# A transformer block on eight cores: a ScalarE copy of the reciprocal row in the weight preparation, and one fewer buffer ahead of the second matmul

## The chip, the cores and the metric

The kernel runs on one Trainium2 chip, as the same program on all 8 cores (two dies, cores 0 to 3 and 4 to 7). Each core takes 4096 tokens: 3967 of the inactive part and 129 of the last 516 of a sequence, in which attention reaches the output. The metric is the device time in microseconds (us) of the slowest core. There is no communication between cores, so each core runs its own program from start to end and the slowest one sets the time.

## What is computed

`x` is 2 x 16384 x 1024. The reference, cut to what matters here:

```python
x = x + layernorm(attention(layernorm(x)))     # 16 heads, 4 sinks + a window of 512
def bitlinear(x, w):
    scale = clip(mean(abs(w), axis=1), 1e-5)
    tern = clip(round(w / scale), -1, 1)
    return x @ (tern * scale).T
h = bitlinear(xn, w_fc) + gate * (xn @ v.T @ fast_b.T @ u.T)   # 1024 -> 4096
r = maximum(h, 0)
x = x + layernorm(bitlinear(r * r, w_proj))                    # 4096 -> 1024
```

## The kernel before

Every engine has its own instruction list, written by hand in program order by the emitter `E`. All instructions are issued from one helper (L114), so the profile shows L114 for nearly all, and the tile names tell the groups apart. `E.gset(key, sem)` notes a semaphore count at which a buffer is free, `E.gwait(eng, key)` makes an engine wait for it. Engines work strictly in the order in which their instructions were emitted. There are two stages.

**Stage 1, to about 1420 us: attention and weight preparation.** After the layer norms of the context, 32 attention units (8 for K, 8 for Q, 16 heads) are emitted, and behind each one two weight preparation units, 64 in all (L824 to L834): 32 of `mk_fc` (L716) for `w_fc`, then 32 of `mk_pj` (L768) for `w_proj`. A unit loads 128 x 1024 weights into one half of `stg`, sums their absolute values in `emit_wsum` (L665: twice a ScalarE Relu into `sgn`, a VectorE pass into `lnscr`, and four matmuls with ones into the PSUM banks `ST` and `pb4`), reduces the sums on VectorE to a row `srowp`, and takes its reciprocal. TensorE then spreads the reciprocal row over 128 partitions into `ST[:, 128:256]` (`mk_pj`: 32 columns), and transposes the scale into `ST[:, 384:385]`. ScalarE copies the scale into `hsc` (`mk_pj`: `osch`), VectorE waits for that copy and multiplies the staged weights in place with the spread row, which it reads from PSUM (L746, L796; `mk_fc` also scales its part of `u2T`, L749). Two more VectorE passes write the ternary weights into `Sfc` or `Spj`. `ST` is noted free behind the multiplication. Next comes the following unit, whose first VectorE pass stands behind all of this on VectorE.

**Stage 2, from about 1420 us: the feed-forward part,** in 16 tiles of 256 tokens. For each of 32 hidden chunks h, f(h) (`emit_fc`, L979) is 8 matmuls `pb<-xn,Sfc` into one of two banks (`pbig0`, `pbig1`), a Relu with scale into `rpp` (ScalarE for even h, VectorE for odd h) and a VectorE multiplication into `r2s`; that frees the bank, so f(h) waits for the multiplication of chunk h-2. p(h) (`emit_proj`, L1016) is 8 matmuls `pb<-r2s,Spj` that add chunk h to four output banks. `r2s` is a ring of 6 buffers and p runs 6 chunks behind f: TensorE's list in a tile is

f(0) to f(3) (`fc_head`, emitted behind the last p of the tile before), f(4), f(5), S, Z, then p(h-6), f(h) for h = 6 to 31, then p(26) to p(31).

S is the 8 matmuls `pb<-fsq,cvecb` of the second layer norm of the tile before; they need `fsq`, which ScalarE and VectorE make from the four output banks of that tile behind its p(31) and behind its followers' chunks 0 to 3 (L1112 to L1146). Z is 4 matmuls `pb<-zrow` of 1 x 512 zeros that clear the output banks (L1071). The rest of the layer norms of the tile before and of the next tile is tied to fixed h: the rows of the second norm at h = 7, its broadcast at 9, its two passes at 11 and 13, the sum with x, the store and the load of `xtl` for the tile after next at 15, the first layer norm of the next tile from h = 18 to 29.

Of the kernel before, what the change touches and what calls it, by code (L numbers as in the profile page):

```python
# [7 lines left out]
F32 = mybir.dt.float32  # L8
BF16 = mybir.dt.bfloat16
AF = mybir.ActivationFunctionType  # L10
ALU = mybir.AluOpType
# [14 lines left out]
TT = 256  # L26
NTILE = TOK // TT
DCN = D // 128
HCN = HF // 128
# [89 lines left out]
def build_nc(n_tiles=NTILE):  # L119
# [29 lines left out]
    with ExitStack() as octx:  # L149
# [7 lines left out]
        srowp = sbuf("srowp", [1, 384], F32)  # L157
        hsc2 = sbuf("hsc2", [128, NFC], F32)
        osch = sbuf("osch", [128, OCN], F32)
        fbTf = sbuf("fbTf", [16, R], F32)  # L160
        fbTg = sbuf("fbTg", [16, R], BF16)
        gatef = sbuf("gatef", [1, 1], F32)
        g2c = sbuf("g2c", [16, 1], F32)
        lnscr = sbuf("lnscr", [128, 4096], BF16)
        zrow = sbuf("zrow", [1, 512], BF16)
        cvec = sbuf("cvecs", [128, 8], F32)
        cvecb = sbuf("cvecb", [128, 8], BF16)
        crow = sbuf("crows", [1, 128], F32)
# [161 lines left out]
        with ExitStack() as actx:  # L330
# [385 lines left out]
            def mk_fc(ph, sg, sgk):  # L716
              def unit():
                slot = ph % 2
                stflat = stg[:, slot * 1024:slot * 1024 + 1024]
                st3 = stg3a if slot == 0 else stg3b  # L720
                E.gwait("sync", f"stg{slot}")
                cL = E.dma("sync", stflat,
                           t_wfc[ph * 128:(ph + 1) * 128, :], f"dS{slot}")
                E.gwait("scalar", sgk)
                E.wait("scalar", f"dS{slot}", cL)
                E.gwait("tensor", "ST")
                cRw = emit_wsum(stflat, sg, 4, 128, 1.0 / D)
                E.wait("scalar", "sV", cRw)
                E.op("scalar", "activation", srowp[0:1, 256:384],
                     srowp[0:1, 0:128], AF.Square, inc="sA")  # L730
                cH2 = E.cnt["sA"]
                E.wait("tensor", "sA", cH2)
                E.op("tensor", "matmul", ST[:, 128:256], crow[:],
                     srowp[0:1, 128:256], start=True, stop=True)
                E.op("tensor", "transpose", ST[:, 384:385],
                     srowp[0:1, 256:384], idf1, inc="sP")
                cBc = E.cnt["sP"]
                E.gset("srowp", "sP")
                E.wait("scalar", "sP", cBc)
                E.op("scalar", "activation", hsc2[:, ph:ph + 1],  # L740
                     ST[:, 384:385], AF.Copy, inc="sA")
                hsc_ready.append(E.cnt["sA"])
                E.wait("vector", "sA", hsc_ready[-1])
                E.wait("vector", "sP", cBc)
                rb3 = ST[:, 128:256].unsqueeze(1).broadcast_to((128, DCN, 128))
                E.op("vector", "tensor_tensor", st3, st3, rb3, ALU.mult)  # L746
                if ph == 0:
                    E.wait("vector", "dGi", c_dG_init)
                E.op("vector", "tensor_tensor",  # L749
                     u2T[0:16, ph * 128:(ph + 1) * 128],  # L750
                     u2T[0:16, ph * 128:(ph + 1) * 128],
                     ST[0:16, 128:256], ALU.mult, inc="sV")
                cZ = E.cnt["sV"]
                E.gset("ST", "sV")
                E.drain("vector")
                E.op("vector", "tensor_single_scalar", sg,
                     stflat, -0.5, ALU.is_lt, inc="sV")
                E.drain("vector")
                E.op("vector", "scalar_tensor_tensor",
                     sfc3[:, :, ph * 128:(ph + 1) * 128], st3, 0.5,  # L760
                     sg.rearrange("p (c t) -> p c t", c=DCN),
                     ALU.is_gt, ALU.subtract, inc="sV")
                sfc_ready.append(E.cnt["sV"])
                E.gset(f"stg{slot}", "sV")
                E.gset(sgk, "sV")
              return unit

            def mk_pj(po, sg, sgk):  # L768
              def unit():
                slot = po % 2  # L770
                stflat = stg[:, slot * 1024:slot * 1024 + 1024]
                stp3 = stflat.rearrange("p (c t) -> p c t", c=HCN)
                E.gwait("sync", f"stg{slot}")
                cL = E.dma("sync", stflat,
                           t_wpj[po * 128:(po + 1) * 128, :], f"dS{slot}")
                E.gwait("scalar", sgk)
                E.wait("scalar", f"dS{slot}", cL)
                E.gwait("tensor", "ST")
                cRw = emit_wsum(stflat, sg, 16, 32, 1.0 / HF)
                E.wait("tensor", "sV", cRw)  # L780
                E.op("tensor", "matmul", ST[:, 128:160], crow[:],
                     srowp[0:1, 128:160], start=True, stop=True)
                E.op("tensor", "transpose", ST[0:32, 384:385],
                     srowp[0:1, 0:32], idf1, inc="sP")
                cBc = E.cnt["sP"]
                E.gset("srowp", "sP")
                E.wait("scalar", "sP", cBc)
                oc = po // 4
                rlo = 32 * (po % 4)
                E.op("scalar", "activation", osch[rlo:rlo + 32, oc:oc + 1],  # L790
                     ST[0:32, 384:385], AF.Copy, inc="sA")
                osch_ready.append(E.cnt["sA"])
                E.wait("vector", "sA", osch_ready[-1])
                E.wait("vector", "sP", cBc)
                rb3 = ST[:, 128:160].unsqueeze(1).broadcast_to((128, HCN, 32))
                E.op("vector", "tensor_tensor", stp3, stp3, rb3, ALU.mult,  # L796
                     inc="sV")
                cZ = E.cnt["sV"]
                E.gset("ST", "sV")
                E.drain("vector")  # L800
                E.op("vector", "tensor_single_scalar", sg,
                     stflat, -0.5, ALU.is_lt, inc="sV")
                E.drain("vector")
                E.op("vector", "scalar_tensor_tensor",
                     spj3[:, :, po * 32:(po + 1) * 32], stp3, 0.5,
                     sg.rearrange("p (c t) -> p c t", c=HCN),
                     ALU.is_gt, ALU.subtract, inc="sV")
                spj_ready.append(E.cnt["sV"])
                E.gset(f"stg{slot}", "sV")
                E.gset(sgk, "sV")  # L810
              return unit
# [99 lines left out]
        with ExitStack() as bctx:  # L911
# [3 lines left out]
            fsq = bsb("fsq", [128, DCN * 512], BF16)  # L915
            fscr = stg
            E.gset("fscr", "sV")
            r2s = [bsb(f"r2s{i}", [128, TT], BF16) for i in range(6)]
            rpp = [bsb(f"rpp{i}", [128, TT], F32) for i in range(2)]

            xn3_t = [v3(x, TT) for x in xn_t]
# [57 lines left out]
            def emit_fc(j, hc):  # L979
# [10 lines left out]
                if hc % 2 == 0:  # L990
# [5 lines left out]
                         bank[:, 0:TT], AF.Relu,  # L996
                         scale=hsc2[:, hc:hc + 1], inc="sA")
                    cR = E.cnt["sA"]
                    E.gwait("vector", f"r2s{hc % 6}")
                    E.wait("vector", "sP", cF)  # L1000
                    E.wait("vector", "sA", cR)
                else:
# [3 lines left out]
                         bank[:, 0:TT], hsc2[:, hc:hc + 1], 0.0,  # L1006
                         ALU.mult, ALU.max)
                    E.drain("vector")
                    E.gwait("vector", f"r2s{hc % 6}")
                E.op("vector", "tensor_tensor", r2s[hc % 6][:],  # L1010
                     bank[:, 0:TT], rpp[hc % 2][:], ALU.mult, inc="sV")
                r2_of[j][hc] = E.cnt["sV"]
                E.gset(key, "sV")
# [2 lines left out]
            def emit_proj(j, hc):  # L1016
                E.wait("tensor", "sV", r2_of[j][hc])
                for oc in range(OCN):
                    bank = pbk[2 + oc // 2]
                    E.op("tensor", "matmul",  # L1020
                         bank[:, (oc % 2) * TT:(oc % 2) * TT + TT],
                         s_pj[:, hc * D + oc * 128:hc * D + oc * 128 + 128],
                         r2s[hc % 6][:], start=False,
                         stop=(hc == HCN - 1 and oc % 2 == 1),
                         inc=("sP" if oc == OCN - 1 else None))
                E.gset(f"r2s{hc % 6}", "sP")

            def fc_head(j):
                r2_of[j] = [0] * HCN
# [31 lines left out]
            ln1 = None  # L1061
            for j in range(n_tiles):
                emit_fc(j, 4)
                emit_fc(j, 5)
                if pend2 is not None:
                    adv(pend2)
                for bnk in range(4):
                    E.gwait("tensor", f"pbproj{bnk}")
                    if j == 0 and bnk == 0:
                        E.wait("tensor", "sV", c_spj)  # L1070
                    E.op("tensor", "matmul", pbk[2 + bnk][:, 0:512],  # L1071
                         zrow[0:1, 0:128], zrow[0:1, 0:512],
                         start=True, stop=False)
                for hc in range(6, HCN):
                    emit_proj(j, hc - 6)
                    emit_fc(j, hc)
                    if pend2 is not None:
                        if hc == 7:
# [25 lines left out]
                            E.gset("fscr", "sV")  # L1104
                            tile_state[j + 1] = ln1[1][0]
                E.gset(f"xn{j % 2}", "sP")
                for hc in range(HCN - 6, HCN):
                    emit_proj(j, hc)
                c_proj = E.cnt["sP"]
                if j + 1 < n_tiles:  # L1110
# [154 lines left out]
```

How the kernel before makes its waits and increments, by code:

```python
    def replay(self, eng_name, engobj, sems):  # L106
        for act in self.q[eng_name]:
            if act[0] == "w":
                engobj.wait_ge(sems[act[1]], act[2])
            elif act[0] == "d":
                engobj.drain()
            else:
                _, fname, args, kwargs, incv = act
                inst = getattr(engobj, fname)(*args, **kwargs)
                if incv is not None:
                    inst.then_inc(sems[incv[0]], incv[1])
```

## Time and profile before

| what | value |
|---|---|
| median of 2 runs | 2811.86 us (2809.02 to 2814.70) |
| profiled execution, its own time | 2807.6 us |
| its span on the slowest core (core 0) | 2806.1 us |
| spans of the other cores | 2768.6 to 2794.7 us |
| mean granted TensorE clock, core 0 | 0.706 (others 0.707 to 0.719) |
| TensorE matmul busy | 1653.1 us, 59% |
| TensorE weight load busy | 1080.6 us, 39% |
| VectorE busy | 1320.2 us, 47% |
| ScalarE busy | 479.3 us, 17% |

The profiled execution took 1.5 us more than its span, and is 4.3 us under the median. The clock is given as a share of 2.4 GHz; it has two levels, 1.0 and 0.5, and a mean between them says how much of a stretch lay at either. In rows of the trace a time in brackets is how long the engine had been idle before the group, with what it waited for. Names in a row are out<-in; `stg<-stg,pb` reads PSUM, `stg<-xtl,stg` reads only SBUF.

### The profile page before, as it was taken

The page shows a single profiled execution, that of the slowest core. Times are in us where ns is not written, and L with a number is a line of the kernel's source. Part 1 is how long each engine was busy: PE and PEld are TensorE (multiplying, and loading weights), DVE is VectorE, ACT ScalarE, POOL GpSimd, SP SyncE. Part 2 cuts the span into 40 slices and gives each one's busy share as a digit, 9 for nine tenths or more (in the row PEclk, how much of TensorE's full clock was granted, in tenths as well). Part 3 has the DMA queues.
Part 4 walks back from the last instruction along what each step waited for, and adds up shares of the span by engine and source line. Part 5 has one row for each costly group of instructions (what it writes and reads, how often), then busy time and mean ns, then how long its engine had stood idle before and what let it go on. Part 6 is the DMA issues. An engine that isn't in the chain of part 4 may idle for free.

```text
span 2806.1 us, 31767 instructions; the slowest of 8 cores (2768.6 to 2806.1 us)
## 1 busy us (share of the span) xinstructions
PE 1653.1 (59%) x10820; PEld 1080.6 (39%) x10824; DVE 1320.2 (47%) x2281; ACT 479.3 (17%) x1025; POOL 20.8 (1%) x36
## 2 busy tenths in 40 slices
PE   3433333333333333334588888888878887878886
PEld 1111111111111111111166656665666665656655
DVE  1244555455545445545444444444544444444544
ACT  1111111111111111121011111111112112111111
POOL 0000000000000000000000000000000000000000
PEclk8555555555555555555588888998999889989988
DMA  2101011101000100001101011100010001110000
GB/s 46 27 30 45 30 45 36 47 30 45 23 31 29 39 23 30 24 29 23 45 1 31 1 31 31 31 25 7 31 31 31 31 1 31 31 31 31 11 22 31
DMA packets 49199, 80.51 MB, mean 29 GB/s; under 512 B 12019, under 2 KB 37748, under 8 KB 48004
## 3 DMA queue, kind: packets, MB, share of 16 engines
q1 hardware_dynamic: 28244, 44.60, 5.4%
q0 software_dynamic: 4160, 17.11, 2.5%
q10 hardware_dynamic: 16640, 16.78, 2.2%
q8 instruction: 92, 1.51, 0.2%
q14 instruction: 63, 0.52, 0.1%
HBM read 70.42 MB, written 16.78 MB: 31 GB/s over the span
## 4 chain that ended last, share of the span: by engine, by line
PE 48%; DVE 27%; issue 9%; ACT 8%; DMA 7%; DVEq 1%; ACTq 0%; SPq 0%; POOLq 0%
PE pb L114 47%; DVE lnscr L114 7%; DVE srowp L114 5%; DMA xtl<-xT 5%; DVE stg L114 4%; DVE srow L114 4%; ACT sgn L114 3%; ACT srow L114 1%; ACT lnscr L114 1%; DVE r2s L114 1%; DVE sgn L114 1%; DVE fsq L114 1%; DVE nmb L114 1%; DVEq L109 1%; DVE Sfc L114 1%
## 5 line engine op out<-in xcount | busy, mean ns | idle before, releaser
L114 PE MATMUL pb<-xn,Sfc 128*128 128x256 bf16 x4096 | 570.0, 287 | 127.9 <-DVE r2s L114 121.3
L114 PE MATMUL pb<-r2s,Spj 128*128 128x256 bf16 x4096 | 561.9, 287 | 0.0
L114 PEld LDWEIGHTS pb<-xn,Sfc 128*128 128x128 bf16 x4096 | 412.0, 103 | 221.8 <-issue 155.0
L114 PEld LDWEIGHTS pb<-r2s,Spj 128*128 128x128 bf16 x4096 | 416.6, 103 | 97.1 <-issue 31.4
L114 DVE TENSOR_TENSOR r2s<-pb,rpp 128x256 bf16<-128x256 f32 x512 | 215.9, 424 | 499.3 <-ACT rpp L114 442.4
L114 PE MATMUL pb<-sgn,cvecb 128*1 128x512 bf16 x256 | 129.5, 609 | 430.2 <-DVE lnscr L114 430.2
L114 DVE SCALAR_TENSOR_TENSOR lnscr<-stg,sgn 128x1024 bf16<-128x1024 f32 x128 | 156.6, 1223 | 297.3 <-ACT sgn L114 297.3
L114 ACT ACTIVATE rpp<-pb,hsc 128x256 f32<-128x256 f32 x256 | 122.1, 477 | 919.7 <-PE pb L114 905.7
L114 PE MATMUL pb<-lnscr,cvecb 128*1 128x512 bf16 x472 | 206.6, 566 | 66.4 <-ACT lnscr L114 65.5
L114 PEld LDWEIGHTS pb<-sgn,cvecb 128*1 128x1 bf16 x256 | 14.5, 80 | 495.0 <-issue 495.0
L114 DVE TENSOR_TENSOR stg<-stg,pb 128x1024 f32<-128x1024 f32 (+1 forms) x96 | 151.1, 1573 | 97.0 <-ACT hsc L114 56.4
L114 ACT ACTIVATE sgn<-stg 128x1024 bf16<-128x1024 f32 x128 | 134.9, 1054 | 316.1 <-PE pb L114 315.6
L114 DVE TENSOR_SCALAR rpp<-pb,hsc 128x256 f32<-128x256 f32 x256 | 122.6, 479 | 88.8 <-PE pb L114 85.8
L114 PE MATMUL pb<-srowp,crows 1*128 1x128 f32 (+1 forms) x128 | 43.6, 437 | 199.9 <-ACT srowp L114 118.6
L114 DVE TENSOR_REDUCE srowp<-pb 1x128 f32<-1x512 f32 (+1 forms) x128 | 81.7, 674 | 136.6 <-PE pb L114 136.6
L114 PEld LDWEIGHTS pb<-srowp,crows 1*128 1x128 f32 x128 | 31.7, 305 | 257.5 <-issue 257.5
L114 PEld LDWEIGHTS pb<-lnscr,cvecb 128*1 128x1 bf16 x472 | 51.8, 113 | 181.3 <-issue 169.4
L114 PE MATMUL pb<-srow,crows 1*128 1x256 f32 (+3 forms) x172 | 59.2, 479 | 94.3 <-DVE srow L114 94.3
L114 PE MATMUL pt<-identb,lnscr 1*128 1x1 bf16 (+3 forms) x160 | 17.5, 232 | 116.5 <-DVE lnscr L114 116.5
L114 PEld LDWEIGHTS pb<-srow,crows 1*128 1x128 f32 x172 | 37.2, 254 | 117.1 <-issue 113.4
L114 DVE TENSOR_TENSOR srow<-srow 1x256 f32<-1x256 f32 (+3 forms) x129 | 46.9, 363 | 58.3 <-ACT srow L114 49.4
L114 DVE TENSOR_SCALAR srow<-pb 1x256 f32<-1x256 f32 (+3 forms) x86 | 27.4, 354 | 94.1 <-PE pb L114 93.9
(102 smaller groups left out, 1208.5 us busy)
## 6 DMA issues: line engine op xcount, KB each, us to landing
stg<-wfc_st SPq DMA_DIRECT2D x32, 512.0 KB, 3.5
stg<-wpj_st SPq DMA_DIRECT2D x32, 512.0 KB, 3.5
outT<-stg ACTq DMA_DIRECT2D x16, 1024.0 KB, 10.2
xtl<-xT SPq DMA_DIRECT2D x16, 512.0 KB, 6.6
xtl<-xT POOLq DMA_DIRECT2D x16, 512.0 KB, 9.8
ctxXg<-ctxT SPq DMA_DIRECT2D x8, 256.0 KB, 2.9
wbuf<-wk POOLq DMA_DIRECT2D x2, 1024.0 KB, 11.1
wbuf<-wq POOLq DMA_DIRECT2D x2, 1024.0 KB, 8.8
```

The costliest lines, as they stand in the source:

```text
L109: engobj.wait_ge(sems[act[1]], act[2])
L114: inst = getattr(engobj, fname)(*args, **kwargs)
```

## The change

In both preparation units ScalarE now also copies the spread reciprocal row from `ST` into a new SBUF buffer `rbb` (two slots of 128 columns), `ST` is noted free behind this copy, and VectorE waits for the copy and reads `rbb` in its multiplications. To have the room (1 KB for each partition), the ring `r2s` goes from 6 buffers to 5, with p running 5 chunks behind f, and `zrow` from 512 to 256 elements, with two matmuls of 256 columns for each bank in Z.

```diff
+        rbb = sbuf("rbb", [128, 256], F32)
-        zrow = sbuf("zrow", [1, 512], BF16)
+        zrow = sbuf("zrow", [1, 256], BF16)
@@ mk_fc
                 E.wait("scalar", "sP", cBc)
+                E.gwait("scalar", f"rbb{slot}")
                 E.op("scalar", "activation", hsc2[:, ph:ph + 1],
                      ST[:, 384:385], AF.Copy, inc="sA")
                 hsc_ready.append(E.cnt["sA"])
-                E.wait("vector", "sA", hsc_ready[-1])
-                E.wait("vector", "sP", cBc)
-                rb3 = ST[:, 128:256].unsqueeze(1).broadcast_to((128, DCN, 128))
+                E.op("scalar", "activation", rbb[:, slot * 128:slot * 128 + 128],
+                     ST[:, 128:256], AF.Copy, inc="sA")
+                cRb = E.cnt["sA"]
+                E.gset("ST", "sA")
+                E.wait("vector", "sA", cRb)
+                rb3 = rbb[:, slot * 128:slot * 128 + 128].unsqueeze(
+                    1).broadcast_to((128, DCN, 128))
                 E.op("vector", "tensor_tensor", st3, st3, rb3, ALU.mult)
...
-                     ST[0:16, 128:256], ALU.mult, inc="sV")
+                     rbb[0:16, slot * 128:slot * 128 + 128], ALU.mult,
+                     inc="sV")
-                E.gset("ST", "sV")
+                E.gset(f"rbb{slot}", "sV")
@@ mk_pj: the same with 32 columns
@@ feed-forward part
-            r2s = [bsb(f"r2s{i}", [128, TT], BF16) for i in range(6)]
+            r2s = [bsb(f"r2s{i}", [128, TT], BF16) for i in range(5)]
...
                 emit_fc(j, 4)
-                emit_fc(j, 5)
...
-                    E.op("tensor", "matmul", pbk[2 + bnk][:, 0:512],
-                         zrow[0:1, 0:128], zrow[0:1, 0:512],
+                    E.op("tensor", "matmul", pbk[2 + bnk][:, 0:256],
+                         zrow[0:1, 0:128], zrow[0:1, 0:256],
                          start=True, stop=False)
-                for hc in range(6, HCN):
-                    emit_proj(j, hc - 6)
+                    E.op("tensor", "matmul", pbk[2 + bnk][:, 256:512],
+                         zrow[0:1, 0:128], zrow[0:1, 0:256],
+                         start=False, stop=False)
+                for hc in range(5, HCN):
+                    emit_proj(j, hc - 5)
                     emit_fc(j, hc)
...
-                for hc in range(HCN - 6, HCN):
+                for hc in range(HCN - 5, HCN):
                     emit_proj(j, hc)
```

TensorE's list around the end of a tile, in the kernel before (`xn,Sfc` are the matmuls of f, `r2s,Spj` those of p, `fsq` is S, `zrow` is Z):

```order
L114 MATMUL pb<-r2s,Spj 128x256 x48
L114 MATMUL pb<-xn,Sfc 128x256 x48
L114 MATMUL pb<-fsq,cvecb 1x512 x8
L114 MATMUL pb<-zrow 128x512 x4
L114 MATMUL pb<-r2s,Spj 128x256 x8
L114 MATMUL pb<-xn,Sfc 128x256 x8
```

and at the same place in the changed kernel:

```order
L114 MATMUL pb<-r2s,Spj 128x256 x40
L114 MATMUL pb<-xn,Sfc 128x256 x40
L114 MATMUL pb<-fsq,cvecb 1x512 x8
L114 MATMUL pb<-zrow 128x256 x8
L114 MATMUL pb<-r2s,Spj 128x256 x8
L114 MATMUL pb<-xn,Sfc 128x256 x8
```

One f, f(5), has moved from ahead of S to behind Z and p(0); behind f(31) there are five p where there were six. VectorE's and ScalarE's lists are unchanged in this stage.

ScalarE's list in the preparation, the difference from the kernel before at two neighbouring `mk_fc` units (`sgn<-stg` are the Relus of `emit_wsum`, `hsc` is the copy of the scale):

```order
 L114 ACTIVATE srowp<-srowp 1x128 [waits sV]
-L114 ACTIVATE hsc<-pb 128x1 [waits sP]
-L114 ACTIVATE sgn<-stg 128x1024 [waits sV,dS1]
-L114 ACTIVATE sgn<-stg 128x1024 [waits sP]
-L114 ACTIVATE srowp<-srowp 1x128 [waits sV]
-L114 ACTIVATE hsc<-pb 128x1 [waits sP]
+L114 ACTIVATE hsc<-pb 128x1 [waits sP,sV]
+L114 ACTIVATE rbb<-pb 128x128
+L114 ACTIVATE sgn<-stg 128x1024 [waits sV,dS1]
+L114 ACTIVATE sgn<-stg 128x1024 [waits sP]
+L114 ACTIVATE srowp<-srowp 1x128 [waits sV]
```

The copy stands between `hsc` and the next unit's Relu, and `hsc` has one more wait, for the slot of `rbb`. On VectorE no instruction is added or moved; its multiplication waits for ScalarE alone where it waited for ScalarE and TensorE.

## Rows read from the trace of the kernel before

**Rows 1.** Part 2 of the page: 40 slices of the span, in tenths.
```profile
PE   3433333333333333334588888888878887878886
PEclk8555555555555555555588888998999889989988
```
**Rows 2.** Timeline, one `mk_fc` unit: start us, us, engine, operation [idle before <-releaser].
```profile
319.32 0.17 ACT L114 ACTIVATE hsc<-pb 128x1 f32<-128x1 f32 x1 [1.01 <-PE pb L114]
...
319.66 1.22 DVE L114 TENSOR_TENSOR stg<-stg,pb 128x1024 f32<-128x1024 f32 x1 [1.75 <-ACT hsc L114]
...
321.97 1.23 DVE L114 SCALAR_TENSOR_TENSOR Sfc<-stg,sgn 128x1024 bf16<-128x1024 f32 x1
323.12 1.22 DVE L114 SCALAR_TENSOR_TENSOR lnscr<-stg,sgn 128x1024 bf16<-128x1024 f32 x1
...
324.58 1.01 PE L114 MATMUL pb<-sgn,cvecb 128*1 128x512 bf16 x2 [5.36 <-DVE lnscr L114]
```
**Rows 3.** Groups by form, VectorE: count | busy us, mean ns | idle before.
```profile
L114 DVE TENSOR_TENSOR stg<-stg,pb 128x1024 f32<-128x1024 f32 x64 | 78.1, 1221 | 94.6 <-ACT hsc L114 56.4 <-ACT osch L114 38.2
L114 DVE TENSOR_TENSOR stg<-stg,pb 128x2048 f32<-128x2048 f32 x32 | 72.9, 2278 | 2.4 <-PE pb L114 2.3
L114 DVE TENSOR_SCALAR sgn<-stg 128x1024 bf16<-128x1024 f32 x64 | 44.4, 694 | 6.8
L114 DVE TENSOR_TENSOR stg<-xtl,stg 128x2048 f32<-128x2048 f32 x16 | 36.7, 2292 | 1.7
L114 DVE TENSOR_TENSOR lnscr<-xtl 128x1024 bf16<-128x1024 f32 x16 | 19.5, 1218 | 0.0
```
**Rows 4.** ScalarE: two neighbours of a timeline, then two groups by form.
```profile
716.75 0.28 ACT L114 ACTIVATE lnscr<-pb 128x129 bf16<-128x129 f32 x1 [1.64 <-PE pb L114]
716.92 1.05 ACT L114 ACTIVATE sgn<-stg 128x1024 bf16<-128x1024 f32 x1
...
L114 ACT ACTIVATE lnscr<-pb 128x64 bf16<-128x64 f32 x64 | 8.2, 198 | 0.0
...
L114 ACT ACTIVATE osch<-pb 32x1 f32<-32x1 f32 x32 | 5.1, 159 | 210.8 <-PE pb L114 210.8
```
**Rows 5.** Timeline across the end of one tile.
```profile
2014.51 5.40 PE L114 MATMUL pb<-r2s,Spj 128*128 128x256 bf16 x48
...
2019.75 1.91 PE L114 MATMUL pb<-xn,Sfc 128*128 128x256 bf16 x16
...
2024.31 2.12 PE L114 MATMUL pb<-xn,Sfc 128*128 128x256 bf16 x16 [0.26 <-DVE r2s L114]
2024.82 0.42 DVE L114 TENSOR_TENSOR r2s<-pb,rpp 128x256 bf16<-128x256 f32 x1 [0.17 <-DVE rpp L114]
2025.16 1.65 DVE L114 TENSOR_SCALAR stg<-pb,osch 128x256 f32<-128x256 f32 x4
...
2029.30 1.89 PE L114 MATMUL pb<-fsq,cvecb 128*1 128x512 bf16 x8 [2.88 <-DVE fsq L114]
2031.12 1.03 PE L114 MATMUL pb<-zrow 1*128 1x512 bf16 x4
2032.09 1.05 PE L114 MATMUL pb<-r2s,Spj 128*128 128x256 bf16 x8
```
**Rows 6.** Chain of waits through the tile behind it: start us, us, what.
```profile
2029.30 7.34 PE pb L114 x52
...
2054.20 2.30 DVE stg L114
...
2057.05 11.98 DMA xtl<-xT
```
**Rows 7.** TensorE in 11.1 us from each S: stretch, length, busy (x), granted clock, DMA.
```profile
1497.80:1508.90 11.10, 11.10 (x43) 0.54 0.00 0
...
1944.60:1955.70 11.10, 11.05 (x58) 0.69 0.01 2
2029.30:2040.40 11.10, 9.95 (x77) 1.00 0.00 0
```

More of the change, by code:

```diff
@@ L787, in unit @@
                 E.wait("scalar", "sP", cBc)
+                E.gwait("scalar", f"rbb{slot}")
                 oc = po // 4
@@ L792, in unit @@
                 osch_ready.append(E.cnt["sA"])
-                E.wait("vector", "sA", osch_ready[-1])
-                E.wait("vector", "sP", cBc)
-                rb3 = ST[:, 128:160].unsqueeze(1).broadcast_to((128, HCN, 32))
+                E.op("scalar", "activation", rbb[:, slot * 128:slot * 128 + 32],
+                     ST[:, 128:160], AF.Copy, inc="sA")
+                cRb = E.cnt["sA"]
+                E.gset("ST", "sA")
+                E.wait("vector", "sA", cRb)
+                rb3 = rbb[:, slot * 128:slot * 128 + 32].unsqueeze(
+                    1).broadcast_to((128, HCN, 32))
                 E.op("vector", "tensor_tensor", stp3, stp3, rb3, ALU.mult,
@@ L798, in unit @@
                 cZ = E.cnt["sV"]
-                E.gset("ST", "sV")
+                E.gset(f"rbb{slot}", "sV")
                 E.drain("vector")
@@ L998, in emit_fc @@
                     cR = E.cnt["sA"]
-                    E.gwait("vector", f"r2s{hc % 6}")
+                    E.gwait("vector", f"r2s{hc % 5}")
                     E.wait("vector", "sP", cF)
@@ L1008, in emit_fc @@
                     E.drain("vector")
-                    E.gwait("vector", f"r2s{hc % 6}")
-                E.op("vector", "tensor_tensor", r2s[hc % 6][:],
+                    E.gwait("vector", f"r2s{hc % 5}")
+                E.op("vector", "tensor_tensor", r2s[hc % 5][:],
                      bank[:, 0:TT], rpp[hc % 2][:], ALU.mult, inc="sV")
@@ L1022, in emit_proj @@
                          s_pj[:, hc * D + oc * 128:hc * D + oc * 128 + 128],
-                         r2s[hc % 6][:], start=False,
+                         r2s[hc % 5][:], start=False,
                          stop=(hc == HCN - 1 and oc % 2 == 1),
                          inc=("sP" if oc == OCN - 1 else None))
-                E.gset(f"r2s{hc % 6}", "sP")
+                E.gset(f"r2s{hc % 5}", "sP")
             def fc_head(j):
```

## The prediction

> **What bounds the kernel now.** I read the page's slices first. They show two stages [rows 1]. For the first 19 of 40 slices TensorE is busy about three tenths of the time at the lower clock level, 1.2 GHz; from then on it is busy eight tenths and the clock is mostly at 2.4 GHz. The change has a part in each, so I price each stage by itself.
>
> In the first stage the timeline of one preparation unit shows a single chain from engine to engine [rows 2]. VectorE's multiplication starts 0.17 us after `hsc` ends (319.32 + 0.17 = 319.49, start 319.66), having been idle 1.75 us. From there VectorE runs without a gap to its pass for the next unit at 323.12, and TensorE waits for that pass. So whatever delays the multiplication delays everything behind it, in the second unit of a pair as shown, and in the first, where the attention unit's VectorE work is queued behind it.
>
> In the second stage I read the timeline across the end of a tile [rows 5]. TensorE runs p(26) to p(31) as 48 matmuls, then f(0) to f(5) in pairs, and is then idle for 2.88 us until `fsq` is ready. That wait does not depend on f(4) or f(5): `fsq` comes from VectorE's evacuation (2025.16), which stands behind the multiplication of chunk 3 (2024.82). Behind S the chain is TensorE up to f(7), then the layer norm's rows, later the sum with x at 2054.20, and a load of `xtl` that ends last [rows 6]. All of these hang on f(7), f(15) and f(18), not on absolute time. Last I read the granted clock in the 11.1 us behind each S [rows 7].
>
> **Part 1: the copy into `rbb`.** It adds 64 ScalarE instructions, each between `hsc` (or `osch`) and the multiplication. On ScalarE a neighbour starts before the one ahead has ended: 716.92 against an end at 716.75 + 0.28 = 717.03, so 0.11 us early [rows 4]. The copy therefore starts 0.17 - 0.11 = 0.06 us after `hsc`. The nearest row in size is the 128x129 copy from PSUM, 0.28 us; the copy ends 0.34 us after `hsc` started, where `hsc` ended after 0.17: +0.17 us for each `mk_fc`, 32 x 0.17 = 5.4 us. For `mk_pj` `osch` takes 0.16, the copy starts 0.05 later, and with 32 columns takes a little under the 0.198 of the 128x64 row, say 0.18: it ends at 0.23, +0.07, 32 x 0.07 = 2.2 us. Together 8 us, all on the chain. VectorE's multiplication loses one of two waits and `hsc` gains one (for the slot, released two units earlier); I count these against each other. Bounds: below, if the whole gap of 0.17 us ahead of the multiplication went with the second wait, 64 x 0.17 = 11 us off, so -3 us. Above, if the copy didn't overlap and took 0.31 and 0.20 us from the end of `hsc` or `osch`, 32 x 0.31 + 32 x 0.20 = 16 us. I take 8, the row nearest in size.
>
> What the copy could give: the multiplication reads SBUF twice instead of SBUF and PSUM. It takes 1221 ns now; a VectorE product of the same size from SBUF alone takes 1218, and at 2048 columns the PSUM form takes 2278 and the SBUF form 2292 [rows 3]. So nothing, within 14 ns x 64 = 1 us. The earlier release of `ST` also gives nothing: the next matmul into `ST` needs VectorE's pass into `lnscr` too, which stands behind the multiplication and two more passes on the same engine [rows 2]. The next unit's Relu is up to 0.2 us later on ScalarE, behind which VectorE is still busy for over 2 us.
>
> The Trainium skill, page "VectorE: DVE Perf Modes", section on the TRN2 errata, gives a VectorE operation a fixed 120 cycles from PSUM and 58 from SBUF. By it, as an estimate, each multiplication would be 0.065 us shorter, about 4 us for 64, and the part would cost 4 us instead of 8. The rows above don't bear it out, so the measured durations stand.
>
> **Part 2: the ring of 5.** Inside a tile it costs nothing: before p(h-5) can come up, f(h-1) has waited for the multiplication of chunk h-3, which is later than h-5, so p never waits; and f(h) still waits for chunk h-2. At the end of a tile p(29) to p(31) come one p earlier behind f(31), but three p's (2.6 us) still lie ahead of p(30).
>
> The cost is at S. With f(5) moved behind it, TensorE reaches S one f earlier and waits longer. One f is 8 matmuls at (2019.75 - 2014.51) / 48 = 0.109 us, 0.87 us [rows 5], so the wait goes from 2.88 to about 3.75 us. From S to f(7) there is now one f and one p more (+1.75 us), from f(31) to the end of p(31) one p fewer (-0.87). Since the norm's steps, the store and the load are tied to f, they all move by 1.75, and nothing in between absorbs it. Net +0.87 us at each of 15 boundaries: 13 us. The first tile has no S and the last S has no f ahead of it.
>
> **Part 3: Z.** Four matmuls take 2032.09 - 2031.12 = 0.97 us now; eight of 256 columns at 0.109 would take 0.87 us [rows 5]. Between -0.1 and, if each added one cost another 0.1, +0.3 us a tile: -2 to +5 us; I take 0.
>
> **Part 4: the clock behind the longer wait.** The 15 stretches of 11.1 us behind S show a granted clock of 1.00 three times, 0.85 to 0.87 twice, 0.69 nine times and 0.54 once; three of the 15 stand in [rows 7]. A mean of 0.69 is (1 - 0.69) / 0.5 = 62% of the stretch at 1.2 GHz, 6.9 us, in which half the work is lost: 3.4 us. TensorE had been idle for 2.88 us ahead of each of them, so a wait of this length sometimes drops the clock and sometimes doesn't, and a longer one can only do so more often. I take two of the three stretches at full clock as lost, 2 x 3.4 = 7 us. Bounds: -7 us, if the phases fall better, to +37 us: a fall to 0.54 at all 15, where 0.54 costs (1 - 0.54) x 11.1 = 5.1 us and the present mean costs (9 x 3.4 + 2 x 1.6 + 5.1) / 15 = 2.6.
>
> The Trainium skill, page "TensorE: Matmul & The Clock Gate", section on HAM oscillation, says that idle gaps between bursts of matmuls put the clock back to its half rate, and that the loss is paid again in each round of a loop. The trace agrees in kind (12 of 15 boundaries). By that rule all 15 would lose, which makes it the rival "clock" below.
>
> **Sum.** 8 + 13 + 0 + 7 = 28 us on the profiled execution's 2807.6 us (span 2806.1 and 1.5 us around it): 2835.6. The median shown lies 4.3 us above that execution, so the forecast is 2840 us, 1.0% over 2811.86.
>
> **The rivals.**
> - *Absorbed.* The moved f costs nothing, because a later wait takes it in, such as the one for the load of `xtl` in the middle of the tile. For it speaks that this load is on the chain with 11.98 us; against it, that it starts behind the sum with x at h = 15, so both ends move [rows 6]. Then only the copy counts: 2812 + 8 = 2820 us.
> - *SBUF is faster.* The multiplication might reach the rate of the one-input row, 694 ns in place of 1221 [rows 3]: 64 x 0.53 = 34 us saved, and with the 28 the time is 2812 + 28 - 34 = 2806 us. Against it stand both SBUF rows with two inputs.
> - *Clock.* The place is S in every tile, the price is the upper bound of part 4. It decides if a wait of 3.75 us drops the clock every time, where one of 2.88 us left it alone at three boundaries of 15, and if the clock then needs as long to come back as at 1497.8: 8 + 13 + 37 = 58 us, 2870 us, 2.1% slower.
> - *No use for the release.* That `ST` is free earlier without anyone who takes it is part of the forecast already; if someone did, it would show as a shorter first stage, with a floor near 2815 us. I give it nothing of its own beyond the range.
>
> **How the numbers follow.** Forecast 0.72, absorbed 0.12, clock 0.10, SBUF faster 0.06. The forecast's own range is 2825 to 2858 (copy -3 to 16 and clock -7 to +20, not all at once). The range for 8 times in 10 takes in the absorbed case and stops short of the clock rival: 2818 to 2864. A measurement of this kernel can tell about 2% (56 us) from no change. Slower by more than that: nearly half of the clock rival and a little of the forecast's tail, 0.07. Faster by more than 2% has no case, 0.01. Within 2%: 0.92.
>
> **What would show it.** Right: a row `rbb<-pb` of 0.28 to 0.31 us x32 and one near 0.18 x32; the multiplication's idle time up from 1.75 to about 1.9 us, its duration still 1.22; TensorE's wait for `fsq` near 3.75 us at 15 boundaries; S to S longer by 0.87 us at equal clock; the stage up to the first Z longer by 8 us. Wrong: a multiplication well under 1.2 us, a wait at S that stays at 2.88, p groups that wait for `r2s`, or a stage 2 as long as before.

## The result and the profile after

The changed kernel takes 2883.04 us (median of 11 runs, 2858.98 to 2923.49) where the kernel before takes 2809.06 us (10 runs): the ratio is 1.0269, with a 95% interval of 1.0227 to 1.0311, 2.7% slower. The forecast was 2840 us, 1.0% slower, and the range ended at 2864; the "clock" rival gave 2870. The ratio is taken without the few executions, such as the one of 2923.49, in which the cores of one die ran longer at a lower granted clock than the other die. The profiled execution of the changed kernel took 2864.0 us and lies near the fast end of its runs, so its trace shows 56 us of the 74 by which the medians differ. On the mean of the eight cores the spans of the two profiled executions differ by 61 us. Pairs of traces are compared below as means over all eight cores where that is said.

The head of the page, which answers to [rows 1]:

```profile
span 2862.5 us, 31962 instructions; the slowest of 8 cores (2823.0 to 2862.5 us)
...
PEclk8555555555555555555588888888888888888888
```

In the second stage no slice reaches nine tenths of the full clock any more, where nine did. The clock in the first stage looks as before.

One preparation unit of core 0, timeline (start us, us, engine, operation, idle before), which answers to [rows 2]:

```profile
306.89 0.17 ACT L114 ACTIVATE hsc<-pb 128x1 f32<-128x1 f32 x1 [1.07 <-PE pb L114]
306.96 0.27 ACT L114 ACTIVATE rbb<-pb 128x128 f32<-128x128 f32 x1
...
307.33 1.23 DVE L114 TENSOR_TENSOR stg<-stg,rbb 128x1024 f32<-128x1024 f32 x1 [1.91 <-ACT rbb L114]
```

The copy starts 0.07 us after `hsc` and takes 0.27 us; the multiplication waits for it, 1.91 us idle in place of 1.75. In three of four units of the second kind (`mk_pj`) the copy starts later than expected:

```profile
710.92 0.16 ACT L114 ACTIVATE osch<-pb 32x1 f32<-32x1 f32 x1 [6.63 <-PE pb L114]
711.10 0.20 ACT L114 ACTIVATE rbb<-pb 128x32 f32<-128x32 f32 x1
711.40 1.23 DVE L114 TENSOR_TENSOR stg<-stg,rbb 128x1024 f32<-128x1024 f32 x1 [1.39 <-ACT rbb L114]
```

Groups by form of core 2, which answer to the first of [rows 3] (count | busy us, mean ns | idle before):

```profile
L114 DVE TENSOR_TENSOR stg<-stg,rbb 128x1024 f32<-128x1024 f32 x64 | 78.4, 1225 | 105.3 <-ACT rbb L114 105.3
...
L114 PE MATMUL pb<-fsq,cvecb 128*1 128x512 bf16 x128 | 57.1, 625 | 65.5 <-DVE fsq L114 60.6 <-ACT stg L114 4.8
```

The multiplication takes 1225 ns, no less than the 1221 from PSUM, and its idle time went from 94.6 to 105.3 us: 11 us for the copy. The second row is S: a mean of 625 ns for one matmul.

The end of a tile on TensorE, core 2, which answers to [rows 5]:

```profile
1511.11 1.03 PE L114 MATMUL pb<-xn,Sfc 128*128 128x256 bf16 x8 [0.25 <-DVE r2s L114]
1516.11 3.57 PE L114 MATMUL pb<-fsq,cvecb 128*1 128x512 bf16 x8 [3.96 <-DVE fsq L114]
1519.61 1.88 PE L114 MATMUL pb<-zrow 1*128 1x256 bf16 x8
1521.43 1.89 PE L114 MATMUL pb<-r2s,Spj 128*128 128x256 bf16 x8
```

The wait ahead of S is 3.96 us where it was 2.88, and S takes 3.57 us where it took 1.89. Behind it Z (1.88) and the first p (1.89) are at half rate too. The stretches of 11.1 us behind S of the same core, which answer to [rows 7] (stretch, length, busy (x), granted clock, DMA):

```profile
1516.11:1527.21 11.10, 11.10 (x56) 0.63 0.00 0
...
2771.30:2782.40 11.10, 11.10 (x52) 0.58 0.01 1
```

All 15 of this core lie between 0.58 and 0.64. Over the eight cores 99 of 120 lie between 0.54 and 0.64 and 21 between 0.85 and 0.88, and none at 1.00. I counted the boundaries of all eight cores, 120 of them, by the time from S to the next norm's broadcast at h = 9. At full clock it is 11.1 us in the order of before (12.86 in the changed order, which has one f and one p more in it). In the kernel before 73 of 120 are longer than that, with a mean of 12.92, so 1.8 us are lost at a boundary. In the changed kernel all 120 are longer, with a mean of 16.61: 3.75 us lost.

Means over eight cores, from S to S: 85.4 us before, 88.8 after, +3.4 for each of 15 boundaries or 50 us. The first Z comes at 1431.5 before and 1439.7 after, +8. Of the 50 us, 13 are the moved f (0.87 each) and 29 are the clock between S and the broadcast (3.75 - 1.82 = 1.93 each). The slow stretch doesn't end there: from the broadcast to the wait for `xtl` it is 24.4 us in place of 23.4, with 2.8 us at half clock in place of 0.7, another 15 us in all. The wait for `xtl`, which comes next, is 4.9 us in place of 5.4 and takes back 7 of them, so 8 are left.

### The profile page after: what moved, and what is told of

Same layout as the page of the kernel before. It is cut to its first block, busy times and chain, and to the rows that moved or that the text cites. A ratio compares the mean times of both kernels' runs of the same rounds, so it can differ in the third digit from the quotient of the medians.

```text
span 2862.5 us, 31962 instructions; the slowest of 8 cores (2823.0 to 2862.5 us)
## 1 busy us (share of the span) xinstructions
PE 1698.6 (59%) x10888; PEld 1109.0 (39%) x10888; DVE 1322.0 (46%) x2281; ACT 487.3 (17%) x1089; POOL 20.8 (1%) x36
## 4 chain that ended last, share of the span: by engine, by line
PE 49%; DVE 27%; issue 9%; ACT 8%; DMA 6%; DVEq 1%; ACTq 0%; SPq 0%; POOLq 0%
PE pb L114 49%; DVE lnscr L114 6%; DVE srowp L114 5%; DMA xtl<-xT 4%; DVE stg L114 4%; DVE srow L114 4%; ACT sgn L114 3%; DMA ctxXg<-ctxT 2%; ACT lnscr L114 1%; ACT srow L114 1%; DVE r2s L114 1%; DVE sgn L114 1%; DVE fsq L114 1%; DVE nmb L114 1%; DVE Sfc L114 1%
## 5 line engine op out<-in xcount | busy, mean ns | idle before, releaser
L114 PE MATMUL pb<-xn,Sfc 128*128 128x256 bf16 x4096 | 583.1, 291 | 101.0 <-DVE r2s L114 95.3
L114 PE MATMUL pb<-r2s,Spj 128*128 128x256 bf16 x4096 | 582.7, 293 | 0.0
L114 PEld LDWEIGHTS pb<-xn,Sfc 128*128 128x128 bf16 x4096 | 420.2, 104 | 197.5 <-issue 123.0
L114 PEld LDWEIGHTS pb<-r2s,Spj 128*128 128x128 bf16 x4096 | 425.1, 105 | 101.2 <-issue 27.7
L114 DVE TENSOR_TENSOR stg<-stg,rbb 128x1024 f32<-128x1024 f32 x64 | 78.4, 1225 | 105.3 <-ACT rbb L114 105.3
L114 PE MATMUL pb<-fsq,cvecb 128*1 128x512 bf16 x128 | 57.1, 625 | 65.5 <-DVE fsq L114 60.6
```

The source lines that it names most:

```text
L114: inst = getattr(engobj, fname)(*args, **kwargs)
```

## The experiments

Two theories were to be told apart. A: the longer wait at S drops the clock every time, and this is most of the loss. Against it stood B (the copy, or the split of Z), C (the new order itself, with waits that follow from it) and later D to F, each told where it is tested. "The wait at S" below is the mean over the 15 boundaries of a core, the same on all eight cores to 0.01 us. A boundary is called long if it takes over half a microsecond more from S to the broadcast than at full clock; that is 11.10 us in the order of before, 12.86 in the changed order, and 11.97 where p alone comes one step earlier (e3, e8, e9). Each ratio is to the kernel before, with its 95% interval. One thing made clean experiments possible: `r2s` lives only in stage 2, whose own buffers need less room for each partition than those of stage 1, so the ring of 6 fits beside `rbb`.

**e1_ring: the shorter ring alone.** Stage 1 and Z are those of the kernel before.

```diff
-            r2s = [bsb(f"r2s{i}", [128, TT], BF16) for i in range(6)]
+            r2s = [bsb(f"r2s{i}", [128, TT], BF16) for i in range(5)]
...
                 emit_fc(j, 4)
-                emit_fc(j, 5)
...
-                    emit_proj(j, hc - 6)
+                    emit_proj(j, hc - 5)
```

Expected: 

> The kernel before with the ring of 5 alone (f(5) behind Z), no copy, Z unsplit. Theory A, the clock falls behind every longer wait at S: most of the loss is here, +50 to +65 us on before, S at half clock (3.57 us) at nearly all 15 boundaries, wait at S 3.9 to 4.0 us. Rival B, the loss comes from the copy or from the split of Z: +13 us at most here.

Measured: 1.0261 (1.0216 to 1.0305). The boundary on core 0:

```profile
2036.92 3.57 PE L114 MATMUL pb<-fsq,cvecb 128*1 128x512 bf16 x8 [3.96 <-DVE fsq L114]
2040.42 1.88 PE L114 MATMUL pb<-zrow 1*128 1x512 bf16 x4
```

All but a few tenths of a per cent of the loss is in this part. The wait is 3.96 us, and all 120 boundaries are longer than at full clock, mean 16.67 us. The loss is 73 us (60 to 85), somewhat above the 50 to 65 that I had written down.

**e2_ring6: the copy and the split Z, with the ring of 6.** The changed kernel with the diff of e1 undone.

```diff
-            r2s = [bsb(f"r2s{i}", [128, TT], BF16) for i in range(5)]
+            r2s = [bsb(f"r2s{i}", [128, TT], BF16) for i in range(6)]
...
                 emit_fc(j, 4)
+                emit_fc(j, 5)
```

Expected: 

> The changed kernel with the ring back at 6 buffers and f(5) ahead of S; the copy and the split Z stay. Theory A: +10 to +15 us on before, wait at S 2.88 us again, S at full clock in some tiles. Rival B (copy or split Z): still +60 us or more.

Measured: 1.0051 (1.0029 to 1.0074), 14 us (8 to 21). The wait at S is 2.91 us, 88 of 120 boundaries are long, mean 13.34 us, and the first Z comes at 1441.3 us (mean of eight cores), 10 us later than before. B falls: what the copy costs is near its 10 us in the first stage, not 60.

**e6_zsplit: the split of Z alone.** The kernel before with two matmuls of 256 columns for each bank.

```diff
-                    E.op("tensor", "matmul", pbk[2 + bnk][:, 0:512],
-                         zrow[0:1, 0:128], zrow[0:1, 0:512],
+                    E.op("tensor", "matmul", pbk[2 + bnk][:, 0:256],
+                         zrow[0:1, 0:128], zrow[0:1, 0:256],
                          start=True, stop=False)
+                    E.op("tensor", "matmul", pbk[2 + bnk][:, 256:512],
+                         zrow[0:1, 0:128], zrow[0:1, 0:256],
+                         start=False, stop=False)
```

Expected: 

> The kernel before with the split of Z alone. All theories: Z takes 0.87 to 1.0 us in place of 0.97 at full clock, no change that can be told (within 5 us of before).

Measured: 1.0000 (0.9970 to 1.0029). Nothing, as said. The wait at S is that of the kernel before, 2.87 us, and yet 86 boundaries are long in this trace against 73: so far apart can two executions be with nothing changed at S.

**e4_fill24_after: the changed kernel, with TensorE kept at work in the wait.** 24 matmuls whose result nobody reads, into the PSUM bank `pt`, which stage 2 leaves unused, are put between f(4) and S. Order, copy and ring stay as changed.

```diff
                 if pend2 is not None:
+                    for _ in range(24):
+                        E.op("tensor", "matmul", ptf[:, 0:TT],
+                             s_fc[:, 0:128], xn_t[j % 2][:, 0:TT],
+                             start=True, stop=True)
                     adv(pend2)
```

Expected: 

> The changed kernel with 24 matmuls of 256 columns into the unused bank pt between f(4) and S, 2.6 us of TensorE work inside the wait. Theory A: the wait left at S is about 1.3 us, the clock stays at 1.0 through S, 45 to 65 us faster than the changed kernel, near +10 to +25 us on before or better. Rival C, the loss is the order itself (one f more behind S) and waits that follow from it, not the clock: no faster than the changed kernel.

Measured: 0.9949 (0.9918 to 0.9979), 3.1% under the changed kernel by the two ratios. Core 0:

```profile
2018.40 2.78 PE L114 MATMUL pt<-xn,Sfc 128*128 128x256 bf16 x24
2022.78 1.89 PE L114 MATMUL pb<-fsq,cvecb 128*1 128x512 bf16 x8 [1.60 <-DVE fsq L114]
2024.60 1.04 PE L114 MATMUL pb<-zrow 1*128 1x256 bf16 x8
```

S starts no earlier, since it waits for `fsq`, but it runs in 1.89 us, and S to the broadcast takes 12.87 us on the mean of 120 boundaries, none of them long. Work was added and 3% went away, some 90 us where 45 to 65 had been expected. C falls, and A is shown: the clock was the cost. The gain passed what A had been given, because the kernel before loses at S as well.

**e4b_fill8_after: the same with 8 matmuls,** as many as f(5) has.

```diff
-                    for _ in range(24):
+                    for _ in range(8):
```

Expected: 

> The changed kernel with 8 such matmuls, as long as one f: the wait at S is back near 2.9 to 3.1 us, with the order of the change. Theory A: the clock behaves as in the kernel before (S at full clock in a fifth to half of the tiles), so the time is before + 10 (copy) + 13 (one f more), some 2830 us. Rival C: as slow as the changed kernel.

Measured: 1.0109 (1.0069 to 1.0149), 31 us (19 to 42) over the kernel before, where 23 had been expected. The wait at S is 3.16 us, 67 of 120 boundaries are long, mean 15.10. Where the clock does fall here, it costs more (4.0 us for a long boundary, 3.0 in the kernel before), as one boundary of core 0 shows:

```profile
2030.48 1.04 PE L114 MATMUL pt<-xn,Sfc 128*128 128x256 bf16 x8
2034.89 2.30 PE L114 MATMUL pb<-fsq,cvecb 128*1 128x512 bf16 x8 [3.37 <-DVE fsq L114]
2037.12 1.88 PE L114 MATMUL pb<-zrow 1*128 1x256 bf16 x8
```

**e3_f5_ahead: the order of TensorE repaired at S, with the ring of 5.** The 8 matmuls of f(5) go back ahead of S; only the VectorE part of chunk 5, which needs the buffer that p(0) frees, stays behind p(0). `emit_fc_mm` is the bank wait and the matmuls of `emit_fc`.

```diff
+            def emit_fc_mm(j, hc):
...
                 emit_fc(j, 4)
+                emit_fc_mm(j, 5)
                 if pend2 is not None:
                     adv(pend2)
```

Expected: 

> The changed kernel, ring of 5, copy and split Z kept, with only the 8 matmuls of f(5) moved back ahead of S (its VectorE work still waits for p(0)). Theory A: the wait at S is 2.88 us again and the time is that of the kernel with the ring of 6, before + 10 to 15 us. Rival D, the fifth buffer itself costs (VectorE waits for p(0), f(7) for VectorE): 10 us or more above the kernel with the ring of 6, and f(7) waits at each boundary.

Measured: 0.9986 (0.9959 to 1.0014). The wait at S is back at 2.91 us on core 0, and 55 of 120 boundaries are long. D falls: the fifth buffer costs nothing that can be told (within 0.3%), even with the copy in the kernel. A had 10 to 15 us over before for it, and it came out 4 under (11 under to 4 over); that made rival F, that p one step earlier is better by itself.

**e8_f5_ahead_nocopy: the same without the copy and with Z unsplit,** so that it differs from the kernel before only in the ring of 5 and in p coming one step earlier.

```diff
-            r2s = [bsb(f"r2s{i}", [128, TT], BF16) for i in range(6)]
+            r2s = [bsb(f"r2s{i}", [128, TT], BF16) for i in range(5)]
...
-                emit_fc(j, 5)
+                emit_fc_mm(j, 5)
```

Expected: 

> The kernel before with the ring of 5, p running 5 chunks behind f, and the matmuls of f(5) kept ahead of S; no copy, Z unsplit. Theory A, only the wait at S matters: same as before within 0.3%. Rival F, p one step earlier is better by itself (the kernel with copy and split Z in this form came out at 0.9986 of before although the copy costs about 10 us): 0.4 to 0.8% faster than before.

Measured: 0.9982 (0.9953 to 1.0011). That is A's answer; of F at most its lower end is left, 0.4% faster, which the interval takes in. The boundaries that are long are fewer, 45 of 120 against 73, and why is open. Open too is where the copy's cost went in e3: its first Z comes at 1443.1 us and here at 1432.2, 11 us apart, but the totals of the two differ by less than their intervals, and in the two traces e3 gets the time back in stage 2, mostly by shorter waits for `xtl` (4.9 against 5.7 us a tile).

**e5_fill24_before: the filler in the kernel before,** 24 matmuls between f(5) and S, with the same diff as e4.

Expected: 

> The kernel before with the 24 matmuls into the unused bank pt between f(5) and S. Theory A: the wait left at S is 0.3 us, S at full clock at 15 boundaries, S to the next rows of the norm 11.1 us everywhere (12.7 to 14.4 now): 25 to 40 us faster than before, 1.0 to 1.4%. Rival C: no change, or slower by the matmuls.

Measured: 0.9916 (0.9874 to 0.9957), 24 us (12 to 35), a little less than the 25 to 40 expected, though the trace shows at S just what was meant: wait 0.25 us, all 120 boundaries at 11.10 us. Core 4:

```profile
2016.89 1.89 PE L114 MATMUL pb<-fsq,cvecb 128*1 128x512 bf16 x8 [0.26 <-DVE fsq L114]
```

The mean loss at S was 1.82 us (12.92 - 11.10), and 15 x 1.82 = 27 us.

**e7_fill3_before: the filler at three waits of the kernel before.** `filler(j, n)` is n such matmuls. Beside the 24 ahead of S, as in e5:

```diff
                     emit_proj(j, hc - 6)
+                    if hc == 21 and j + 1 < n_tiles:
+                        filler(j, 36)
                     emit_fc(j, hc)
...
                         elif hc == 27:
+                            filler(j, 24)
                             adv(ln1[0])
```

Expected: 

> The same, with 36 more such matmuls ahead of f(21), where TensorE waits for the load of xtl, and 24 ahead of the broadcast of the first norm's rows at h = 27. Theory A: the half-clock stretches behind these two waits go as well, 1.5 to 3 us each a tile: another 25 to 60 us, 2.5% or more below before in all. Rival E: the longer dense load on all cores brings a lower granted clock on its own, or the load of xtl is already there in some tiles and the 36 matmuls are in the way: no better than with the filler at S alone.

Measured: 0.9688 (0.9647 to 0.9729), 2706 us, 3.1% faster than before and some 64 us under e5, where 25 to 60 had been expected. Core 0 at the wait for `xtl` and at S, and the page's clock:

```profile
2019.92 4.09 PE L114 MATMUL pt<-xn,Sfc 128*128 128x256 bf16 x36
2025.93 1.03 PE L114 MATMUL pb<-xn,Sfc 128*128 128x256 bf16 x8 [1.92 <-DVE r2s L114]
...
2062.52 2.78 PE L114 MATMUL pt<-xn,Sfc 128*128 128x256 bf16 x24
2065.56 1.89 PE L114 MATMUL pb<-fsq,cvecb 128*1 128x512 bf16 x8 [0.26 <-DVE fsq L114]
```

```profile
PEclk7555555555555555555559999999999999999998
```

The waits for `xtl` and for the rows are still there in length, only filled; what is gone is the half clock behind them. From S to S a tile takes 79.1 us on the mean of the cores, where the kernel before has 85.4. E, that the denser load lowers the granted clock by itself or that the fillers get in the way, falls: no slice of stage 2 but the last is under nine tenths.

**e9_fill3_ring5: e7 on the kernel of e8.** The three fillers, with the ring of 5 and f(5)'s matmuls ahead of S.

```diff
                 emit_fc_mm(j, 5)
                 if pend2 is not None:
+                    filler(j, 24)
                     adv(pend2)
...
                     emit_proj(j, hc - 5)
+                    if hc == 21 and j + 1 < n_tiles:
+                        filler(j, 36)
```

Expected: 

> That kernel with the three fillers (24 ahead of S, 36 ahead of f(21), 24 at h = 27). Theory A: as the kernel of six buffers with the fillers, 0.969 of before, within 0.2%. Rival F: clearly below it, 0.963 or less.

Measured: 0.9661 (0.9616 to 0.9706), 2703 us. A had 0.969 within 0.2% and F 0.963 or less; it lies between, and can't be told from e7. These two are the fastest versions of the study, and both beat the kernel before and the changed one.

The wait at S, the long boundaries of 120 in each trace, and the mean time that a boundary lost against full clock:

| kernel | mean wait at S, us | long ones | mean loss, us | ratio to before |
|---|---|---|---|---|
| e5_fill24_before | 0.25 | 0 | 0.0 | 0.9916 |
| e4_fill24_after | 1.42 | 0 | 0.0 | 0.9949 |
| before | 2.87 | 73 | 1.8 | 1 |
| e6_zsplit | 2.87 | 86 | 2.2 | 1.0000 |
| e8_f5_ahead_nocopy | 2.87 | 45 | 1.4 | 0.9982 |
| e2_ring6 | 2.91 | 88 | 2.2 | 1.0051 |
| e3_f5_ahead | 2.91 | 55 | 1.5 | 0.9986 |
| e4b_fill8_after | 3.16 | 67 | 2.2 | 1.0109 |
| e1_ring | 3.95 | 120 | 3.8 | 1.0261 |
| changed kernel | 4.04 | 120 | 3.75 | 1.0269 |

Between 2.87 and 3.16 us the number doesn't follow the wait, so in that region something else decides with it, which was not found out. The means hide a detail: in the kernels with the copy the wait is 0.26 to 0.36 us longer than its usual value at two or four of the 15 boundaries, the same ones on all eight cores, because VectorE starts to evacuate the banks that much later; in the kernels without the copy it never is. Why is open.

## Why the prediction was wrong

**What bounds the kernel** held. The chain in a preparation unit, the wait at S as the place where the ring costs, and the norm's steps that move with f all show in the traces as said.

**Part 1, the copy: right in mechanism, a little small.** 8 us said, with bounds of -3 and 16; 11 us more idle time ahead of the multiplication on core 0, 8 to 12 us by the first Z. For a usual `mk_fc` unit it was 0.16 us (0.17 said). For `mk_pj` it was 0.07, as said, in 8 of the 32 units, and 0.21 in nearly all others: there `osch` and the copy behind it didn't overlap, 711.10 against an end at 711.08. The multiplication from SBUF at 1225 ns gave nothing back. The 4 us that I had estimated from the Trainium skill's page "VectorE: DVE Perf Modes", section on the TRN2 errata, for the SBUF source are not there.

**Part 2, the moved f: right in kind.** The wait grew by 1.16 us on the mean (2.87 to 4.04), not by 0.87. Of this 1.08 come from the order (e1: 3.95), since f(5) had itself waited 0.21 us for the multiplication of chunk 3 (its pair takes 2.12 us where the pair before the waits takes 1.91), and so had covered more of the wait than its own matmuls. The other 0.08 are the longer waits at four boundaries that only kernels with the copy have. The net cost of 0.87 us a tile, 13 us, is right at full clock: S to the broadcast at full clock is 12.86 in place of 11.10 (+1.76, said 1.75), and behind f(31) one p fewer. But part of it can be taken in: between e4 and e5, in which no boundary lost the clock in either order, a tile differs by 0.45 us only (83.76 and 83.31 from S to S), with a wait for `xtl` of 4.9 against 5.2 us, and the ratios differ by 0.33%, 9 us with the copy in it. Inside a tile no p group waited for `r2s`, on any core, and e3 and e8 show no cost of the ring of 5 where f(5) stays ahead of S. So "absorbed" was wrong for the whole of it in the order as changed, and a better order was there to be had.

**Part 3, Z: right,** by e6.

**Part 4, the clock: the step that failed.** "I take two of the three stretches at full clock as lost, 2 x 3.4 = 7 us." In its place all 120 boundaries lost time, and each lost 3.75 us where the mean had been 1.82: 15 x 1.93 = 29 us from S to the broadcast, and 8 more behind it, 37 us in place of 7. The working had three faults. It read the granted clock of one core, core 0, on which 12 of 15 boundaries were already slow, so that hardly any seemed left to lose; over eight cores it was 73 of 120. It took the depth of a fall from the present mean, when the longer wait also left more at half clock: a long boundary lost 3.0 us before and 3.75 after, and S itself went from partly to wholly slow (over 3.5 us at 96 of 120 boundaries, where none was before). By these figures 18 of the 29 us are more boundaries and 11 are deeper falls. And it priced 11.1 us behind S only, while the slow stretch now runs on past the broadcast, where it costs the 15 us of which the wait for `xtl` takes 7 back. So the upper bound of +37 us was met, but by luck: its own term, the 11.1 us behind S, came to 29, and the rest is a term that the working didn't have. The case that stood behind it, with 0.10, was the one that came true in kind.

**The rivals.** "Clock" gave 2870 and had the mechanism and the place, and nearly the price; e4 shows it, by taking nothing away but the idle time. The median of 2883 is still 13 us over it. The profiled execution of the changed kernel was 19 us under the median of its runs (2864.0 against 2883.04), where that of the kernel before was 1.5 under (2807.6 against 2809.06), and this part of the 74 us isn't in any trace. "SBUF is faster" fell with the 1225 ns.

By the Trainium skill, page "TensorE: Matmul & The Clock Gate", section on HAM oscillation, idle gaps between bursts of matmuls put the clock down to half rate, and the loss comes back with each round. Where the wait was 4 us the trace agrees at 120 boundaries of 120; where it was 1.4 us none of 120 lost anything. I had quoted this rule, and gave it a tenth.

## What to carry to other kernels

Where TensorE waits in every round of a loop and its clock is mixed behind the wait, look for an edge. Here 1.1 us more wait in each of 15 rounds cost 73 us (e1), nearly 5 us a round, and idle time filled with matmuls that nobody reads cost nothing that shows and gave back 24 us (e5) and some 90 (e4). Read the granted clock behind each repeated wait on all cores, and price a longer wait with every round slow, not with the present share. Before a buffer is cut to make room, look which stage has the memory peak, and what is reordered with it: here the ring could have stayed at 6 (e2), or f(5)'s matmuls alone could have stayed where they were (e3).

## What the runs showed that was not expected

The kernel before loses 27 us at S and more behind two other waits in each tile, and 84 idle-filling matmuls for each of 15 tile ends make it 3.1% faster (1260 matmuls more, 2706 us in place of 2800). On ScalarE, a copy from PSUM into 128 partitions starts 0.10 us before the one ahead ends, if that one also wrote 128 partitions (306.89 + 0.17 against 306.96; 31 of 32 units on each core). If the one ahead wrote 32 partitions, it depends on which: 0.09 us of overlap where these were the first 32, as in each fourth `mk_pj` unit (8 of 8), and a gap of 0.02 us where they lay higher (23 of 24). Nothing else was found that sets the two kinds of unit apart, but no run was made to test it.
